# A pipelined attention kernel: where the probabilities are normalised, the row shape of two groups of matmuls, another order and prologue

## The chip, the core and the metric

One core of a Trainium2 chip. The number is the device time of one execution in microseconds; for the kernel before it is the median of three runs.

## The reference, cut to what matters

Two layers on 128 sequences of 64 rows and 256 features, all in float32. What the change touches:

```
x_mod = rms(x) * (1 + scale_a) + shift_a ;  q, k, v = split(x_mod @ qkv_w)
q, k  = rope(rms(q)), rope(rms(k))
attn  = softmax(q k^T / 4)                      # 16 heads of 16 features, 64 x 64
x    += gate_a * ((attn @ v) @ proj_w + proj_b)
x    += gate_m * ((silu(h @ w1) * (h @ w3)) @ w2)        # 704 hidden features
self  = [x, cond] @ W_self + b_self             # cond left out for rows whose sum is 0
out   = self + two graph attentions (20 keys, masked, with an edge bias)
y     = x + relu(out)
```

## The kernel before

A block is four sequences (256 rows, two tiles of 128); there are 32. Each engine runs its own list of steps (ORDER, line 83 on) once an iteration; an entry `(a, step, n)` works on block m + a, so three blocks ahead are under way at once. The lists are unrolled for the first iterations (-3 to 0) and the last three, and looped by `Fori` for 28 in between (`run_steps`). Engines meet by semaphores alone: `wait` for data, `wait_free` for a PSUM bank whose last reader must have gone. BANK says which of the eight PSUM banks each step writes.

Products with weights take three float32r terms for float32's precision: high part by low weight, high by high, low by high. ACT makes the high part (`nh`, `gh`, `aoh`), POOL or DVE the low one (`nl`, `gl`, `aol`); all these matmuls are issued at L486.

First attention, per tile: `score` (L587) into four banks, DVE takes the row maximum (L1151) and subtracts it (L1156), ACT makes the exponential (L897), PE transposes the unnormalised probabilities eight times (`probs_t`, L607), ACT copies them (L904, L906), and `mix` (L622) multiplies by v. v has two columns of ones per pair of heads, so the sums come out beside the result; DVE inverts them (L1162) and scales (L1165) into `aon`, PE transposes that back to features by rows (`mix_t`, L631), and ACT and DVE split it for `proj`. The second attention sums and inverts ahead of its transposes (L1267, L1271, POOL's multiply L1379), and its mix (L806) gives features by rows directly.

The MLP's hidden features are five whole chunks of 128 and a half one. `mlp_down` takes four chunks first and then chunk five and the half one, whose three terms are matmuls on partitions 64 to 127 (L696). Then DVE multiplies by the gate (L1206), POOL adds the residual (L1360), ACT and POOL split it, and `self` follows; it ends in `self_cond`, two matmuls of `cond_rows` (8 partitions) with `gate` (8 partitions, L1212).

POOL also does the first norm's root and power (L1303, L1305), the scaling by the modulation, the block-diagonal keys (L1327) and the residual of the first layer (L1356).

The prologue (line 1004 on) makes the modulation and the condition's product on PE into banks 0 to 3, splits the latter on DVE (L1065, L1067), and makes the rope tables; PE and POOL start their lists only after `mods_set` has reached 6, which is that split.

## Time and profile before

| | |
|---|---|
| median of 3 runs | 1424.35 us (1419.06 to 1425.61) |
| profiled execution | 1418.18 us, span 1416.1 us |
| PE busy | 1342.2 us, 95% |
| DVE busy | 1135.2 us, 80% |
| ACT busy | 878.6 us, 62% |
| POOL busy | 712.1 us, 50% |
| TensorE clock granted | 0.977 of full speed on average |

The span runs from the first to the last instruction. Busy is the union of the instructions' times of one engine; a matmul's time includes its way through the array, so neighbouring matmuls overlap, and what one costs is seen from start to start.

### The profile page before, as it was taken

How to read it: one execution, taken by the hardware profiler on the slowest of the kernel's cores; microseconds unless marked ns; L12 is line 12 of the kernel's file. 1: busy time of each engine (PE TensorE's matmuls, PEld its weight loads, DVE VectorE, ACT ScalarE, POOL GpSimd, SP SyncE). 2: the span in 40 equal slices, each digit the busy share in tenths (PEclk: the TensorE clock that was granted, in tenths of full speed). 3: DMA queues.
4: the chain of work that ended last, by engine and by line, in shares of the span. 5: the costliest groups of instructions: out<-in, count | busy, mean ns of one | idle time of the engine just before them, and what ended most of it. 6: DMA issues, size and time to landing. Idle time of an engine off the chain costs nothing.

```text
span 1416.1 us, 51305 instructions
## 1 busy us (share of the span) xinstructions
PE 1342.2 (95%) x20276; PEld 1229.1 (87%) x20276; DVE 1135.2 (80%) x2033; ACT 878.6 (62%) x1752; POOL 712.1 (50%) x612
## 2 busy tenths in 40 slices
PE   4679999999999999999999999999999999999985
PEld 3578899999998999999898999999999999999974
DVE  5667888888888888888888888888888888888753
ACT  4556666666666666666666666666666666656542
POOL 0235555455655544555555455555545555554541
PEclk8589999999999999999999999999999999999998
DMA  7001111010111101111110111111011111100100
GB/s 240 29 23 30 45 43 43 18 38 30 43 43 43 43 15 36 34 43 43 43 43 15 35 35 43 43 43 43 15 33 37 43 43 43 43 15 28 30 22 16
DMA packets 49827, 56.19 MB, mean 40 GB/s; under 512 B 4352, under 2 KB 47744, under 8 KB 49792
## 3 DMA queue, kind: packets, MB, share of 16 engines
q1 hardware_dynamic: 48944, 53.86, 12.1%
q10 hardware_dynamic: 848, 1.84, 0.4%
q8 instruction: 25, 0.41, 0.1%
q14 instruction: 10, 0.08, 0.0%
...
## 4 chain that ended last, share of the span: by engine, by line
PE 73%; issue 9%; POOL 7%; ACT 3%; DVE 1%; ACTq 0%; POOLq 0%; DVEq 0%
PE psum L486 39%; PE psum L607 5%; PE psum L622 5%; PE psum L728 4%; PE psum L792 4%; PE psum L758 4%; PE psum L775 3%; POOL nl L1315 3%; PE psum L587 3%; PE psum L806 2%; POOL gl L1315 2%; POOL kbd L1327 2%; ACT gh L926 1%; PE psum L534 1%; ACT qkT L892 1%
## 5 line engine op out<-in xcount | busy, mean ns | idle before, releaser
L1315 POOL TENSOR_TENSOR gl<-gf,gh 128x512 fp32r<-128x512 f32 x96 | 124.3, 1295 | 260.4 <-ACT gh L926 260.4
L486 PE MATMUL psum<-nh,w_lo 128*128 128x256 f32 x704 | 182.2, 289 | 0.0
L486 PE MATMUL psum<-nh,w_hi 128*128 128x256 f32 x704 | 176.8, 282 | 0.0
L1315 POOL TENSOR_TENSOR nl<-xn,nh 128x512 fp32r<-128x512 f32 x64 | 99.2, 1551 | 127.3 <-ACT nh L864 127.3
L486 PEld LDWEIGHTS psum<-nh,w_lo 128*128 128x128 f32 x704 | 132.8, 189 | 1.0 <-issue 1.0
L486 PEld LDWEIGHTS psum<-nh,w_hi 128*128 128x128 f32 x704 | 133.0, 189 | 0.0
L1379 POOL TENSOR_TENSOR e<-e,inv 128x640 f32<-128x640 f32 x64 | 82.0, 1282 | 87.6 <-DVE inv L1271 87.6
L486 PE MATMUL psum<-nl,w_hi 128*128 128x256 f32 x704 | 115.4, 282 | 0.0
L926 ACT ACTIVATE gh<-gf 128x512 fp32r<-128x512 f32 x96 | 60.3, 628 | 61.6 <-DVE gf L1201 60.8
L486 PEld LDWEIGHTS psum<-nl,w_hi 128*128 128x128 f32 x704 | 97.5, 188 | 0.0
L486 PE MATMUL psum<-qkv_lo,nh 128*128 128x512 f32 (+1 forms) x256 | 88.5, 356 | 2.8 <-ACT nh L864 2.8
L946 ACT ACTIVATE sf<-psum,colb 128x256 f32<-128x256 f32 x64 | 26.8, 470 | 103.3 <-PE psum L486 103.3
L1151 DVE TENSOR_REDUCE mx<-psum 128x16 f32<-128x1024 f32 x64 | 78.1, 1221 | 14.4 <-PE psum L587 14.1
L911 ACT ACTIVATE aoh<-psum 128x512 fp32r<-128x512 f32 x32 | 19.1, 598 | 109.2 <-PE psum L631 109.2
L486 PE MATMUL psum<-gh,w_lo 128*128 128x256 f32 x320 | 83.0, 290 | 1.3 <-ACT gh L926 1.3
L486 PE MATMUL psum<-qkv_hi,nh 128*128 128x512 f32 (+1 forms) x256 | 82.4, 343 | 0.0
L607 PE MATMUL psum<-ident,e 128*128 128x128 f32 x512 | 77.9, 289 | 4.3 <-ACT e L897 4.2
L1360 POOL TENSOR_TENSOR x<-x 128x512 f32<-128x512 f32 x32 | 41.5, 1296 | 78.2 <-DVE x L1206 78.2
L1327 POOL TENSOR_TENSOR kbd<-qkT,hmask 128x512 f32<-128x512 f32 x64 | 66.5, 1041 | 28.0 <-ACT qkT L892 28.0
L486 PE MATMUL psum<-gh,w_hi 128*128 128x256 f32 x320 | 79.6, 279 | 0.0
L1156 DVE TENSOR_TENSOR e<-psum,mx 128x1024 f32<-128x1024 f32 x64 | 78.0, 1218 | 1.3
L622 PEld LDWEIGHTS psum<-vb,pT 128*64 128x64 f32 x2048 | 66.6, 140 | 12.8 <-issue 12.5
...
## 6 DMA issues: line engine op xcount, KB each, us to landing
...
```

The lines of the kernel that those rows point to most:

```text
L486: last = nc.tensor.matmul(out, lhsT, rhs, start=start and i == 0, stop=stop and i == len(terms) - 1)
L607: last = nc.tensor.transpose(pT_out[t][j // 4][:, j % 4, :], e0[t][:, 2 * pair(j):2 * pair(j) + 2, :].rearrange("p h s -> p (h s)"), ident ...
L622: last = nc.tensor.matmul(mix_ps[t][s * S:(s + 1) * S, j, :], pT0[:, j, s * S:(s + 1) * S], vb[:, t, s, j, :], start=True, stop=True, tile ...
L728: last = nc.tensor.matmul(k1_out[:, k, :].rearrange("p (b k) -> p b k", b=MB), wk1[:, c, k * P:(k + 1) * P], sf[:, c, :].rearrange("p (b s ...
L758: last = nc.tensor.matmul(v1_out[r * NKP:(r + 1) * NKP, b, :], kv[:, c, b, :], wo1[:, c, r * P:(r + 1) * P], start=c == 0, stop=c == DC - ...
L792: last = nc.tensor.transpose(pT1_out[t][j // 4][:, j % 4, :], e1[t][:, 2 * pair(j):2 * pair(j) + 2, :, :].rearrange("p h a k -> p (h a k)" ...
L926: nc.scalar.activation(gh[:, 2 * n:2 * n + 2, :], gf[:, :, :], ACT.Copy).then_inc(g_hi.sem, 1)
L1151: nc.vector.tensor_reduce(mx0_v, s_v[t], AX.X, ALU.max).then_inc(maxima.sem, 1)
L1156: nc.vector.tensor_tensor(e0_v[t], s_v[t], mx0_v.unsqueeze(3).to_broadcast([P, NG, 4, S]), ALU.subtract).then_inc(shifted_s.sem, 1)
L1315: return nc.gpsimd.tensor_tensor(out, full, hi.bitcast(F32), ALU.subtract)
L1327: nc.gpsimd.tensor_tensor(kbd[:, t, :, :, :, :].rearrange("p c s h k -> p (c s) h k"), qkT[t][:, 1, :, :].rearrange("p c (s k) -> p (c s) ...
L1379: nc.gpsimd.tensor_tensor(e_v, e_v, inv1[t][:, :].unsqueeze(2).to_broadcast([P, ND * H, NKV]), ALU.mult)\
```

## The change

The first attention's exponentials are summed on DVE and inverted (`soft0`, `soft0_inverse`), POOL multiplies them in place, and PE transposes the finished probabilities; ACT copies the transposes over `e0`, so each tile has its own buffer, and waits for all eight transposes first. `mix` has the second attention's form: output by features, the transposes of `mix_t` and the two columns of ones are gone. The MLP's half chunk holds the low part of g in its first 64 partitions (POOL writes it there) and w2's last 64 rows twice, so its terms are ordinary matmuls on 128 partitions. `gate` and `cond_rows` have 128 partitions, the rest of them zero. The second attention's score bias is one instruction a tile. Banks and the orders of all engines are different. In the prologue PE and POOL no longer wait for the condition's split ahead of the lists, and DVE makes it and the tables behind the first block's shift. The diff, cut (of the old orders, PE's and POOL's stand):

```diff
-    "xT": 6, "qk": (2, 3), "v": (7, 1), "heads": (7, 5), "probsT": (5, 4, 4, 0), "probsT1": (0, 5, 4, 7),
-    "mix": (5, 6), "q1": (4, 6), "score": 0, "score1": 0, "mixT": 6, "proj": 2, "norm1": 7, "up": (6, 4, 6),
-    "gate": (3, 1, 0), "down": 1, "rowsum": 3, "self": 4, "k1": 5, "v1": 7, "mix1": 5,
+    "xT": 2, "qk": (6, 3), "v": (4, 1), "heads": (0, 2), "probsT": (3, 4, 0, 5), "probsT1": (7, 1, 3, 4),
+    "q1": (0, 4), "score": 3, "score1": 1, "proj": 1, "norm1": 7, "up": (5, 7, 4), "gate": (6, 3, 0), "down": 5,
+    "rowsum": 7, "self": 0, "k1": 1, "v1": 0, "mix1": 6, "mix": 2,
...
     "PE": [
-        (2, "heads", 1), (1, "proj", 0), (0, "self", 0), (0, "self_cond", 0), (2, "score", 0), (0, "k1", 0),
-        (0, "q1", 0), (1, "norm1_mean", 0), (0, "q1", 1), (1, "norm1_apply", 0), (2, "probsT", 0),
-        (3, "norm0_apply", 0), (0, "score1", 0), (0, "v1", 0), (2, "mix", 0), (2, "probsT", 1), (1, "mlp_up", 0),
-        (1, "mlp_up", 1), (3, "qkv", 0), (0, "probsT1", 0), (2, "mix", 1), (3, "qkv", 1), (0, "mix1", 0),
-        (0, "probsT1", 1), (1, "mlp_up", 2), (0, "mix1", 1), (1, "mlp_down", 0), (1, "mlp_down", 1), (2, "mixT", 0),
-        (3, "heads", 0),
+        (2, "heads", 1), (0, "mlp_down", 1), (1, "proj", 0), (2, "score", 0), (0, "self", 0), (0, "self_cond", 0),
+        (3, "norm0_apply", 0), (1, "norm1_mean", 0), (0, "k1", 0), (0, "q1", 0), (1, "norm1_apply", 0), (0, "q1", 1),
+        (0, "v1", 0), (0, "score1", 0), (1, "mlp_up", 0), (2, "probsT", 0), (1, "mlp_up", 1), (2, "probsT", 1),
+        (3, "qkv", 0), (2, "mix", 0), (2, "mix", 1), (3, "qkv", 1), (1, "mlp_up", 2), (0, "probsT1", 0),
+        (1, "mlp_down", 0), (0, "probsT1", 1), (3, "heads", 0), (0, "mix1", 0), (0, "mix1", 1),
     ],
     "DVE": [
...
+        (1, "norm1_mean", 0), (3, "norm0_apply", 0), (2, "score", 1), (0, "k1", 0), (2, "soft0", 0),
+        (1, "norm1_apply", 0), (2, "soft0_inverse", 0), (1, "norm1_shift", 0), (3, "norm0_shift", 0), (2, "soft0", 1),
+        (1, "edges", 0), (2, "soft0_inverse", 1), (0, "score1_bias", 0), (0, "score1_bias", 1), (0, "score1_max", 0),
+        (1, "mlp_up", 0), (0, "score1", 0), (0, "score1_max", 1), (0, "score1", 1), (0, "soft1", 0),
+        (0, "soft1_inverse", 0), (1, "mlp_up", 1), (3, "qkv", 0), (0, "soft1", 1), (0, "soft1_inverse", 1),
+        (3, "qkv", 1), (1, "mlp_up", 2), (3, "rope_scale", 0), (3, "rope", 0), (3, "rope", 1), (2, "mixT", 0),
+        (0, "mix1", 0), (0, "out", 0), (1, "mlp_down", 0), (1, "edge_masks", 0), (2, "proj", 0), (3, "score_max", 0),
+        (1, "row_mask", 0), (3, "score", 0), (2, "norm1_squares", 0), (3, "score_max", 1),
     ],
     "Activation": [
...
+        (0, "x2_split", 0), (3, "norm0_mean", 0), (1, "norm1_mean", 0), (0, "self", 0), (0, "self_split", 0),
+        (0, "keys", 0), (2, "score", 0), (0, "q1", 0), (2, "score", 1), (0, "q1", 1), (1, "norm1_apply", 0),
+        (3, "norm0_apply", 0), (1, "mlp_up", 0), (0, "v1", 0), (2, "probsT", 0), (1, "mlp_split", 0),
+        (0, "score1", 0), (1, "mlp_up", 1), (1, "edges", 0), (2, "probsT", 1), (0, "score1", 1), (3, "qkv", 0),
+        (1, "mlp_split", 1), (3, "qkv", 1), (2, "mixT", 0), (1, "mlp_up", 2), (3, "rope_scale", 0), (0, "probsT1", 0),
+        (1, "mlp_split", 2), (0, "probsT1", 1), (3, "heads", 0), (3, "heads", 1),
     ],
     "Pool": [
-        (1, "proj", 0), (0, "self_split", 0), (3, "norm0_mean", 0), (1, "norm1_mean", 0), (1, "norm1_scale", 0),
-        (3, "norm0_scale", 0), (1, "norm1_apply", 0), (3, "norm0_apply", 0), (0, "soft1", 0), (1, "mlp_up", 0),
-        (0, "soft1", 1), (1, "edges", 0), (1, "mlp_up", 1), (1, "mlp_up", 2), (1, "mlp_down", 0), (3, "heads", 0),
-        (1, "x2_split", 0), (3, "heads", 1),
+        (0, "mlp_up", 2), (2, "heads", 0), (2, "heads", 1), (0, "mlp_down", 0), (0, "x2_split", 0), (1, "proj", 0),
+        (3, "norm0_mean", 0), (3, "norm0_scale", 0), (0, "self_split", 0), (1, "norm1_mean", 0),
+        (1, "norm1_scale", 0), (1, "norm1_apply", 0), (2, "soft0", 0), (2, "soft0", 1), (3, "norm0_apply", 0),
+        (1, "mlp_up", 0), (1, "edges", 0), (0, "soft1", 0), (1, "mlp_up", 1), (0, "soft1", 1),
     ],
     "SP": [
-        (0, "self", 0), (3, "norm0_mean", 0), (1, "mlp_up", 0), (3, "norm0_scale", 0), (2, "norm0_apply", 0),
+        (1, "norm0_apply", 0), (3, "norm0_mean", 0), (1, "mlp_up", 0), (0, "self", 0), (3, "norm0_scale", 0),
         (0, "out", 0),
...
-        inv0 = [sb(f"inv0_{i}", [P, NJ, 2]) for i in range(TILES)]
-        aon = [sb(f"aon{i}", [P, NJ, 2, DH]) for i in range(TILES)]
+        sum0 = sb("sum0", [P, H])
+        inv0 = [sb(f"inv0_{i}", [P, H]) for i in range(TILES)]
         pT = sb("pT", [P, 2, NJ, P])
-        pT0, pT1 = pT[:, 0, :, :], pT[:, 1, :, :]
+
+        pT0 = [v[:, :, :].rearrange("p h s -> p (h s)").rearrange("p (j t) -> p j t", t=P) for v in e0]
+        pT1 = [pT[:, t, :, :] for t in range(TILES)]
...
+        mods_banks = [bank for i, bank in enumerate(banks) if i != BANK["xT"]][:4]
...
-        mix_ps = [banks[b][:, 0:NJ * (2 * DH + 2)].rearrange("p (j f) -> p j f", j=NJ) for b in BANK["mix"]]
-        aoT_ps = banks[BANK["mixT"]]
+        mix_ps = halves(BANK["mix"])
+        aoT_ps = banks[BANK["mix"]]
...
-            pe.wait_ge(mods_set.sem, 6)
-            pe.wait_ge(mods_set_a.sem, NMOD - 4)
...
+                if isinstance(m, int) and m == 0:
+                    pe.wait_ge(mods_set.sem, 6)
+                    pe.wait_ge(mods_set_a.sem, NMOD - 4)
...
-                wait(pe, exps, m, t + 1)
+                wait(pe, probs0, m, t + 1)
...
-                        last = nc.tensor.matmul(mix_ps[t][s * S:(s + 1) * S, j, :], pT0[:, j, s * S:(s + 1) * S],
-                                                vb[:, t, s, j, :], start=True, stop=True, tile_position=(0, s * S))
+                        f = 32 * (j % 4)
+                        last = nc.tensor.matmul(mix_ps[f:f + 32, j // 4, t * P + s * S:t * P + (s + 1) * S],
+                                                vb[:, t, s, j, :], pT0[t][:, j, s * S:(s + 1) * S],
+                                                start=True, stop=True, tile_position=(0, f))
                 last.then_inc(mixed.sem, 1)
-
...
-            def mix_t(m, n):
-                wait(pe, mix_normed, m, TILES)
-                wait_free(pe, m, (z_silu, -1, 3), (mix_normed, 0, 2))
-                for c in range(DC):
-                    for t in range(TILES):
-                        last = nc.tensor.transpose(aoT_ps[:, c * MT + t * P:c * MT + (t + 1) * P],
-                                                   aon[t][:, c * 4:(c + 1) * 4, :, :].rearrange("p j h f -> p (j h f)"),
-                                                   ident[:, :])
-                last.then_inc(aoT_done.sem, 1)
...
                     linear(down_ps[:, o, :], low_terms("w2", out_chunks[o], gl, [MC - 2]), False, False)
+
                 for o in both:
-                    for i, (w, a) in enumerate(((wl["w2"], gh), (wh["w2"], gh), (wh["w2"], gl))):
-                        last = nc.tensor.matmul(down_ps[:, o, :], w[half, MC - 1, out_chunks[o]], a[half, MC - 1, :],
-                                                start=False, stop=o == DC - 1 and i == 2, tile_position=(HALF, 0))
+                    last = linear(down_ps[:, o, :], high_terms("w2", out_chunks[o], gh, [MC - 1]), False, o == DC - 1)
                 last.then_inc(down_done.sem, 1)
 
...
-                wait(act, pT_ps, m, 2 * t + 1)
-                wait(act, mixed, m, t)
-                nc.scalar.activation(pT0[:, 0:4, :], pT_out[t][0], ACT.Copy).then_inc(pT_a.sem, 1)
                 wait(act, pT_ps, m, 2 * t + 2)
-                nc.scalar.activation(pT0[:, 4:8, :], pT_out[t][1], ACT.Copy).then_inc(pT_b.sem, 1)
+                nc.scalar.activation(pT0[t][:, 0:4, :], pT_out[t][0], ACT.Copy).then_inc(pT_a.sem, 1)
+                nc.scalar.activation(pT0[t][:, 4:8, :], pT_out[t][1], ACT.Copy).then_inc(pT_b.sem, 1)
 
             def mix_t(m, n):
...
+            def cond_and_tables():
+                dve.wait_ge(mods_ps.sem, NMOD + 1)
+                nc.vector.tensor_copy(cond_hi[:, :], mods_banks[3][:, 0:D]).then_inc(mods_set.sem, 1)
+                dve.wait_ge(mods_set.sem, 5)
+                nc.vector.tensor_tensor(cond_lo[:, :], mods_banks[3][:, 0:D], cond_hi[:, :].bitcast(F32), ALU.subtract).then_inc(mods_set.sem, 1)
+                dve.wait_ge(mods_set.sem, 6)
+                dve.wait_ge(sines.sem, 1)
...
+                low_parts(*LOW_PARTS["norm0_shift", 0])
...
-            def mix(m, t):
-                wait(dve, mixed, m, t + 1)
-                nc.vector.reciprocal(inv0[t][:, :, :], mix_ps[t][:, :, 2 * DH:2 * DH + 2]).then_inc(inv_sums.sem, 1)
-                wait(dve, inv_sums, m, t + 1)
-                wait_last(dve, aoT_done, m)
-                nc.vector.tensor_tensor(aon[t][:, :, :, :], mix_ps[t][:, :, 0:2 * DH].rearrange("p j (h f) -> p j h f", h=2),
-                                        inv0[t][:, :, :].unsqueeze(3).to_broadcast([P, NJ, 2, DH]), ALU.mult)\
-                    .then_inc(mix_normed.sem, 1)
+            def soft0(m, t):
+                wait(dve, exps, m, t + 1)
+                wait(dve, inv_sums, m, t)
+                nc.vector.tensor_reduce(sum0[:, :], e0[t][:, :, :], AX.X, ALU.add).then_inc(sums0.sem, 1)
+
+            def soft0_inverse(m, t):
+                wait(dve, sums0, m, t + 1)
+                nc.vector.reciprocal(inv0[t][:, :], sum0[:, :]).then_inc(inv_sums.sem, 1)
 
             def mix_t(m, n):
...
-                for a in range(ND):
-                    nc.vector.tensor_tensor(
-                        e1[t][:, :, a, 0:NKV].rearrange("p (r h) k -> p r h k", r=NG),
-                        s1_ps[t].rearrange("p r (a h k) -> p r a h k", a=ND, k=NKV)[:, :, a, :, :],
-                        edge_bias[:, t, a * NKV:(a + 1) * NKV].unsqueeze(1).unsqueeze(1).to_broadcast([P, NG, 4, NKV]), ALU.add)\
-                        .then_inc(biased1.sem, 1)
+                nc.vector.tensor_tensor(
+                    e1[t][:, :, :, 0:NKV].rearrange("p (r h) a k -> p r h a k", r=NG), s1_v[t],
+                    edge_bias[:, t, :].rearrange("p (a k) -> p a k", a=ND).unsqueeze(1).unsqueeze(1).to_broadcast([P, NG, 4, ND, NKV]),
+                    ALU.add).then_inc(biased1.sem, 1)
...
-            pool.wait_ge(mods_set.sem, 6)
...
-                low_part(gl[:, 2 * n:2 * n + 2, :], gf[:, :, :], gh[:, 2 * n:2 * n + 2, :]).then_inc(g_lo.sem, 1)
+                if n < MC // 2 - 1:
+                    low_part(gl[:, 2 * n:2 * n + 2, :], gf[:, :, :], gh[:, 2 * n:2 * n + 2, :]).then_inc(g_lo.sem, 1)
+                else:
+
+                    low_part(gl[:, 2 * n, :], gf[:, 0, :], gh[:, 2 * n, :]).then_inc(g_lo_whole.sem, 1)
+                    wait(pool, g_lo_whole, m, 1)
+                    low_part(gh[0:HALF, 2 * n + 1, :], gf[HALF:, 1, :], gh[HALF:, 2 * n + 1, :]).then_inc(g_lo.sem, 1)
+                    wait(pool, g_lo, m, n + 1)
...
+            def soft0(m, t):
+                wait(pool, inv_sums, m, t + 1)
+                nc.gpsimd.tensor_tensor(e0[t][:, :, :], e0[t][:, :, :], inv0[t][:, :].unsqueeze(2).to_broadcast([P, H, S]), ALU.mult)\
+                    .then_inc(probs0.sem, 1)
...
-        "w2": np.insert(a["L0_cond_w2_w"], [HM - HALF] * HALF, 0, 0),
+        "w2": np.concatenate([a["L0_cond_w2_w"], a["L0_cond_w2_w"][HM - HALF:]], 0),
```

## Rows read from the trace of the kernel before

**Rows 1.** The page: busy us, share of the span, instructions.

```profile
PE 1342.2 (95%) x20276; PEld 1229.1 (87%) x20276; DVE 1135.2 (80%) x2033; ACT 878.6 (62%) x1752; POOL 712.1 (50%) x612
```

**Rows 2.** Windows: busy us (instructions) of each engine, clock, DMA share, GB/s.

```profile
701.20:742.60 41.40, 41.13 (x635) 37.68 (x633) 34.78 (x63) 26.96 (x54) 22.34 (x20) 1.00 0.12 36
```

**Rows 3.** PE's time line over one block: start us, us, line, instruction.

```profile
701.17 0.38 PE L541 MATMUL psum<-ident,rms_inv 128*128 128x128 f32 x2
...
706.22 1.13 PE L622 MATMUL psum<-vb,pT 128*64 128x34 f32 x32
707.28 1.32 PE L607 MATMUL psum<-ident,e 128*128 128x128 f32 x8
...
720.60 0.81 PE L806 MATMUL psum<-pT,vb 128*32 128x64 f32 x32
721.33 1.09 PE L792 MATMUL psum<-ident,e 128*128 128x128 f32 x8
...
742.55 0.38 PE L541 MATMUL psum<-ident,rms_inv 128*128 128x128 f32 x2
```

**Rows 4.** The same time line, from the MLP's tail to k1.

```profile
729.05 0.38 PE L696 MATMUL psum<-gh,w_lo 64*128 64x256 f32 x1
...
729.92 0.66 PE L631 MATMUL psum<-ident,aon 128*128 128x128 f32 x4
730.42 1.04 PE L570 MATMUL psum<-ident,qr 128*128 128x128 f32 x8
731.43 0.38 PE L486 MATMUL psum<-aoh,proj_lo 128*128 128x256 f32 x1
...
733.02 0.50 PE L486 MATMUL psum<-nh,ones_r 128*128 128x256 f32 x2
...
734.20 0.28 PE L486 MATMUL psum<-nh,self_hi 128*128 128x256 f32 x1
734.59 0.50 PE L486 MATMUL psum<-nl,ones_r 128*128 128x256 f32 x2
734.93 0.64 PE L486 MATMUL psum<-nl,self_hi 128*128 128x256 f32 x4
735.68 0.49 PE L486 MATMUL psum<-gate,cond_rows 8*128 8x256 f32 x2
736.22 1.20 PE L587 MATMUL psum<-kbd,qkT 32*64 32x128 f32 x64
737.34 2.01 PE L728 MATMUL psum<-sf,wk 128*128 128x80 f32 x16
```

**Rows 5.** DVE's groups: busy us, mean ns of one, idle before and releaser.

```profile
L1151 DVE TENSOR_REDUCE mx<-psum 128x16 f32<-128x1024 f32 x64 | 78.1, 1221 | 14.4 <-PE psum L587 14.1
...
L1248 DVE TENSOR_TENSOR e<-psum,edge_bias 128x320 f32<-128x320 f32 x128 | 56.3, 482 | 8.3 <-PE psum L775 8.3
...
L1165 DVE TENSOR_TENSOR aon<-psum,inv 128x256 f32<-128x256 f32 x64 | 27.2, 424 | 2.4 <-DVE inv L1162 0.2
...
L1162 DVE RECIPROCAL inv<-psum 128x16 f32<-128x16 f32 x64 | 16.3, 254 | 49.0 <-PE psum L622 48.8
```

**Rows 6.** Time line of DVE and POOL behind the MLP's end, same block.

```profile
730.24 0.68 DVE L1206 TENSOR_TENSOR x<-psum,mods 128x512 f32<-128x512 f32 x1
...
731.00 1.29 POOL L1360 TENSOR_TENSOR x<-x 128x512 f32<-128x512 f32 x1 [2.45 <-DVE x L1206]
...
739.97 0.95 POOL L1305 TENSOR_TENSOR rms_inv<-rms_root,minus_half 128x2 f32<-128x2 f32 x1
```

**Rows 7.** POOL's groups: its multiply of the second attention.

```profile
L1379 POOL TENSOR_TENSOR e<-e,inv 128x640 f32<-128x640 f32 x64 | 82.0, 1282 | 87.6 <-DVE inv L1271 87.6
```

**Rows 8.** L1130 alone over one block: ns min/median/max, first and last start.

```profile
L1130 DVE TENSOR_TENSOR qr<-qc,qs x4: 410/416/1024, 720.9 to 724.4; 128x256 f32<-128x256 f32 x4
```

**Rows 9.** Time line of POOL and DVE at its first two.

```profile
720.30 1.29 POOL L1315 TENSOR_TENSOR gl<-gf,gh 128x512 fp32r<-128x512 f32 x1 [1.36 <-ACT gh L926]
720.85 1.36 DVE L1130 TENSOR_TENSOR qr<-qc,qs 128x256 f32<-128x256 f32 x2
```

**Rows 10.** Time line: POOL's first instruction of its list.

```profile
19.67 0.20 POOL L1303 TENSOR_TENSOR rms_root<-x_ms,eps 128x2 f32<-128x2 f32 x1 [19.22 <-DVE cond_lo L1067]
```

More of the change, by code:

```diff
@@ L88 @@
     ],
     "DVE": [
-        (2, "rope", 0), (2, "rope", 1), (0, "mlp_down", 0), (1, "mixT", 0), (1, "proj", 0), (0, "row_mask", 0),
-        (0, "edge_masks", 0), (2, "score_max", 0), (2, "score", 0), (1, "norm1_squares", 0), (2, "score_max", 1),
[4 rows of a table removed]
-        (1, "mlp_up", 1), (2, "mix", 1), (3, "qkv", 0), (3, "qkv", 1), (1, "mlp_up", 2), (0, "mix1", 0),
-        (1, "edges", 0), (3, "rope_scale", 0), (0, "out", 0),
[5 rows of a table added]
+        (3, "qkv", 1), (1, "mlp_up", 2), (3, "rope_scale", 0), (3, "rope", 0), (3, "rope", 1), (2, "mixT", 0),
@@ L98 @@
+        (0, "mix1", 0), (0, "out", 0), (1, "mlp_down", 0), (1, "edge_masks", 0), (2, "proj", 0), (3, "score_max", 0),
+        (1, "row_mask", 0), (3, "score", 0), (2, "norm1_squares", 0), (3, "score_max", 1),
     ],
     "Activation": [
-        (2, "rope_scale", 0), (0, "mlp_split", 2), (1, "mixT", 0), (2, "heads", 0), (2, "heads", 1),
-        (0, "x2_split", 0), (0, "self", 0), (1, "norm1_mean", 0), (0, "keys", 0), (0, "self_split", 0),
-        (3, "norm0_mean", 0), (2, "score", 0), (0, "q1", 0), (0, "q1", 1), (2, "probsT", 0), (2, "score", 1),
@@ L509, in _ @@
             for c in range(DC):
-                last = nc.tensor.matmul(banks[3][:, 0:D], cond[:, c, :], w_cond[:, c, :], start=c == 0, stop=c == DC - 1)
+                last = nc.tensor.matmul(mods_banks[3][:, 0:D], cond[:, c, :], w_cond[:, c, :], start=c == 0, stop=c == DC - 1)
             last.then_inc(mods_ps.sem, 1)
@@ L811, in _ @@
             run_steps(pe, "PE", {
-                "norm1_mean": norm1_mean, "norm0_apply": norm0_apply, "norm1_apply": norm1_apply, "qkv": qkv, "heads": heads, "score": score, "probsT": probs_t, "mix": mix, "mixT": mix_t, "proj": proj,
+                "norm1_mean": norm1_mean, "norm0_apply": norm0_apply, "norm1_apply": norm1_apply, "qkv": qkv, "heads": heads, "score": score, "probsT": probs_t, "mix": mix, "proj": proj,
                 "mlp_up": mlp_up, "mlp_down": mlp_down, "self": self_feat, "self_cond": self_cond, "k1": k1,
@@ L1011, in _ @@
             nc.vector.memset(vb1[:, :, :, :].rearrange("p b f j -> p (b f j)"), 0.0).then_inc(zeros_set.sem, 1)
+            for v in (gate, cond_rows):
+                last = nc.vector.memset(v[:, :].bitcast(F32), 0.0)
+            last.then_inc(zeros_set.sem, 1)
             for v in e1:
                 last = nc.vector.memset(v[:, :, :, :].rearrange("p h a k -> p (h a k)"), 0.0)
-            last.then_inc(zeros_set.sem, 1)
-            dve.wait_ge(zeros_set.sem, 5)
-            for h in range(2):
-                last = nc.vector.memset(vb[h * S:(h + 1) * S, :, :, :, 2 * DH + h:2 * DH + h + 1], 1.0)
             last.then_inc(zeros_set.sem, 1)
@@ L1112, in _ @@
             half = DH // 2
+            def cond_and_tables():
[5 more added lines that the diff above has]
+                dve.wait_ge(sines.sem, 1)
+                for i in range(2):
+                    for a in range(2):
+                        nc.vector.tensor_tensor(cosw[:, i, a * half:(a + 1) * half], lnw[:, i, a * half:(a + 1) * half],
+                                                ang[:, 1, :], ALU.mult)
+                        last = nc.vector.scalar_tensor_tensor(sinw[:, i, a * half:(a + 1) * half], ang[:, 0, :],
+                                                              (1.0, -1.0)[a], lnw[:, i, a * half:(a + 1) * half],
+                                                              ALU.mult, ALU.mult)
+                last.then_inc(table_step.sem, 1)
+                dve.wait_ge(table_step.sem, 9)
+                low_parts(*LOW_PARTS["norm0_shift", 0])
             def qkv(m, t):
@@ L1153, in score @@
             def score(m, t):
-                wait(dve, pT_ps, m, 2 * (t + 1 - TILES))
+                wait(dve, mixed, m, t + 1 - TILES)
                 wait(dve, maxima, m, t + 1)
@@ L1333, in norm0_scale @@
             def norm0_scale(m, n):
+                if isinstance(m, int) and m == 0:
+                    pool.wait_ge(mods_set.sem, 4)
                 wait(pool, xT_in_s, m, 16)
```

152 lines of the change are left out of this document (66 added, 86 removed), and 4 rows, old and new, of the table ORDER.

## The prediction, made before the changed kernel ran

> **What bounds the kernel now.** I read the page's busy line first: PE is busy 95% of the span, DVE 80%, POOL 50% [rows 1]. That alone doesn't say that PE is the limit, because ends of matmuls are modelled. So I read the table by windows in the middle: in 41.40 us PE is busy 41.13, DVE 34.78, ACT 26.96, POOL 22.34 at full granted clock [rows 2]. Then the time line of PE: the same instruction of two successive blocks (L541) starts at 701.17 and at 742.55, so one block of four sequences takes 41.38 us [rows 3], and between those two marks PE issues almost without a hole. The other engines have about 6.6 us (DVE) or more to spare in every block. The kernel is thus 32 times 41.4 us of PE's instruction stream plus about 92 us of filling and draining the pipeline. What takes PE instructions away pays one for one, as long as nothing that PE waits for comes later than its turn.
>
> PE's pace is read from a group in the time line: four matmuls of 256 columns in 0.64 us, one alone 0.28, so (0.64 - 0.28) / 3 = 0.12 us from start to start [rows 4].
>
> **What the change takes off PE, per block.**
> (a) The transposes of the mixed output (mixT) go: L631 starts at 729.92 and what follows it at 730.42 [rows 4]: 0.50 us.
> (b) The mix keeps its 16 matmuls a tile but takes the form that the second attention's mix has already (32-column weights, 64 moving columns). The old form runs from 706.22 to 707.28 = 1.06 us, the form taken over from 720.60 to 721.33 = 0.73 us [rows 3]. Twice 0.33 = 0.66 us.
> (c) The tail of the MLP's second product: six matmuls on 64 rows run from 729.05 to 729.92 = 0.87 us [rows 4]; four on whole rows at PE's pace are 0.48: 0.39 us. Entering and leaving the 64-row form costs something on top, see below; I take 0.47.
> (d) The condition's matmuls on 8 rows: 735.68 to 736.22 = 0.54 us for two instructions whose pace gives 0.24 [rows 4]. Whatever follows has an entry too, so I take 0.20 of the 0.30 (bounds 0 and 0.30).
> Sum 1.83 us. In (c) and (d) the time line shows that a group with another number of rows starts and ends some 0.1 us late. The Trainium skill says why (TensorEngine Tiling (Array Packing), Key Properties): a change of the tiling mode drains the engine. By that rule the new order should give a little more, since it also puts the two mixes of each attention side by side (two pairs of switches fewer); I leave that out of the sum.
> Before, PE also stood still twice in this stretch: the pace puts the low ones_r matmuls at 734.32 and they start at 734.59; four matmuls from 734.93 should end at 735.41 and the gated ones start at 735.68 [rows 4]. That is 0.54 us. PE without any wait would then take 41.38 - 0.54 - 1.83 = 39.0 us a block.
>
> **What it puts on the other engines, per block.**
> DVE: two reciprocals and two multiplies of the old normalisation go, 2 x (0.254 + 0.424) = 1.36 us. Two sums of 128x1024 come; the nearest row is the maximum over the same shape, 1.221 us, and the two reciprocals are 0.254 again: 2.95 us [rows 5]. The sum reads SBUF and not PSUM; bounds 1.1 and 1.3 each. The bias of the second attention becomes one instruction of 640 elements instead of two of 320 at 0.482; in between the rows of 256 and 1024 elements (0.424 and, for 1024, 1.221) it is about 0.82: -0.3 us for both tiles (bounds -0.5 and +0.3, as its reading of PSUM has more dimensions). DVE goes from 34.8 to 36.1 us.
> POOL: two multiplies of 128x1024 by a broadcast column. The same operation at 640 elements takes 1.282 us [rows 7], so 2.05 by its rate (bounds 1.3 and 2.6). With the split of one low part in two, about +4.2 us: 22.3 becomes 26.5.
> ACT: its copies of the transposed probabilities are the same in number and size: nothing. SP: the order of five loads changes, all small beside the block; no cost.
> Both rises are hidden as long as DVE (36.1) and POOL (26.5) stay under PE, with 3 to 4 us to spare on DVE where there were 6.6.
>
> The cover is not free of traps, because POOL and DVE disturb each other. L1130, two halves of the rotation, takes 0.410 us at best and 1.024 at worst in the same block; the long one starts at 720.85, inside a POOL subtraction that runs from 720.30 to 721.59 [rows 8, 9]. The Trainium skill's SBUF page (SBUF — State Buffer, Who interferes with whom) has the rule: a DVE instruction with two SBUF inputs and a GpSimd instruction that reads SBUF exclude each other for the whole instruction. Here the trace agrees. By it the two new POOL multiplies of 2.05 us each can hold up such a DVE instruction for up to 2.05 us. By the same rule the new sums (one input) are never held up. In the new order POOL runs them after the first part of norm1's low parts, while DVE has mostly sums, maxima and PSUM readers; the first DVE operation with two SBUF inputs behind them is the subtraction in score1, which I expect to be held up by under 1 us. That eats DVE's reserve and not PE's time.
>
> **Where PE will wait.** I followed the new orders from one mlp_down to the next. In most places what PE needs is 0.4 to 3 us early (probabilities of tile 0: about 1.2 us early; rope before heads: little, but early). One stretch is not covered. Old order between the last product of the MLP and k1: mixT, heads, proj, self, self_cond, score. New order: proj, score, self, self_cond, norm0_apply (block 3 ahead), norm1_mean, k1. Count from the start s of the last tail matmul.
> The chain to self: PE's end and hand-over 0.33, DVE 0.68, POOL's addition 1.29, ACT's split; POOL starts at 731.00, its end is 732.29, and PE's self starts at 733.02 [rows 4, 6], so ACT and the hand-overs are 0.73. With 0.08 between DVE and POOL self can start at s + 3.11. PE has only proj (731.43 to 733.02, 1.59) and score (736.22 to 737.34, 1.12) [rows 4] and the tail matmul's 0.12 to do: s + 2.83. Wait 0.28, as heads no longer stand there.
> The chain to self_cond: rowsum's low matmuls end, DVE compares, PE gets the gate: 734.59 to 735.68 before, 1.09; PE has the 0.34 + 0.48 of its own [rows 4]: wait 0.27, as before.
> The chain to norm0_apply: on POOL, behind x2's low part (1.24), come the residual's addition (as the 1.29 of rows 6, 1.24 from start to start) and the root and power of norm0, about 0.3 and 0.95 [rows 6]; the power is less where DVE leaves the port free. From s + 3.1: 3.1 + 1.24 + 1.24 + 0.3 + (0.7 to 0.95) = s + 6.6 to 6.8. PE has finished self_cond at s + 5.75 (3.11, high parts 1.30, low parts and gate 1.09, two matmuls 0.24). Wait 0.85 to 1.1. k1 is just ready after it.
> Sum of waits 1.4 to 1.65; block 39.0 + 1.5 = 40.5, and 40.3 if the spared switches count. I take 40.4: 1.0 us less than now.
>
> **Filling and draining.** POOL's first instruction waits until 19.67 us for the condition's low part [rows 10]; afterwards it waits only for what it reads, and PE can spread at once behind its first matmuls (about 18.7). So the first normalised block is some 2 us earlier. Against that, in the filling blocks the sum, the reciprocal and POOL's multiply (1.2 + 0.25 + 2.05) stand on the open chain where before 0.25 + 0.42 and the transposes did. I take -2 for the filling (bounds -5 and +4) and -1 for the draining.
>
> **Sum.** The loop's 28 blocks and the one ahead of it: 29 x 1.0 = 29 us, and 3 more: 32 off. The profiled execution took 1418.18 us (span 1416.1): 1386 for its like. It lies 6.2 under the median of the runs, 1424.35, so the median should be about 1392.
>
> **Rivals.**
> Dense: the waits don't come (POOL reaches norm0's root earlier, or x2's chain is faster than I have it). Then a block takes 39.0 and 29 x 2.4 + 3 = 72 us go: 1352. For it: rows 3 and 4 show how little PE waits today although the same engines feed it. Against: the chain to norm0_apply is made of durations that are all in the trace. Chance 0.18.
> Nothing: a second unforeseen wait of about 1 us a block stands beside the three (the likeliest is probabilities of the first tile: POOL's 2.05 at its upper bound, held up by DVE's shifts): 40.4 + 1.0, so 1420 to 1424. Chance 0.08.
> Slower: DVE becomes the bound. Its 6.6 us without work may be waits that stay, and not a reserve, and work of 1.3 us plus up to 2.05 us of being shut out by POOL's two multiplies, once a block, come on top: 34.8 + 6.6 + 1.3 + 0.9 to 2.05 = 43.6 to 44.8, at least 2 us a block over now, 29 x 2.2 = 64: 1488. In a mild form, where half of the idle time is used, 1440. The point from which it decides is DVE over 41.4 us a block. For it: L1130 [rows 8]. Against: DVE's idle pieces are many and most of its new work stands in front of them. Chance 0.10.
> My own case has 0.64.
>
> **The numbers.** The range from 1352 to 1418 leaves out about 1 in 10 on each side. This kernel's measurement can tell about 0.5% (7 us) from no change: faster 0.82, same 0.08, slower 0.10.
>
> **What would show it.** In the changed profile L541's like repeats every 40.4 us; the mix takes 0.73, the tail 0.5; no L631; PE waits once for the power of norm0 (0.85 to 1.1) and once for x2's split (0.3); DVE 36.1 of 40.4 and POOL 26.5. Wrong: a repeat under 39.5 (my chain is too long), over 41 (a wait that I don't see), or DVE without any idle time.

## Result: slower, 1457.8 us against a forecast of 1392

The changed kernel takes 1457.78 us (median of 4 runs, 1448.58 to 1460.17) where the kernel before takes 1423.18: a ratio of 1.0235 (95% interval 1.0191 to 1.0279). The forecast was 1392 us, its range ended at 1418. The change makes the kernel slower, clear of no change. The profiled execution has a span of 1446.5 us instead of 1416.1; it is the fastest of the changed kernel's, so the loss read from it below is rather too small.

The page of the changed kernel, busy line (compare [rows 1]):

```profile
PE 1313.8 (91%) x20084; PEld 1236.7 (85%) x20084; DVE 1210.0 (84%) x1969; ACT 884.6 (61%) x1752; POOL 836.3 (58%) x708
```

PE has less to do, as forecast, and is a smaller share of a longer span. The chain of work that ended last, with its shares of the span, names on its page what wasn't there before:

```profile
PE 74%; DMA 7%; DVE 4%; issue 3%; ACT 1%; POOL 1%; SPq 1%; DVEq 0%; ACTq 0%; POOLq 0%
PE psum L492 44%; PE psum L723 7%; DMA cond_rows<-cond_parts 6%; PE psum L753 4%; PE psum L787 4%; PE psum L614 4%; PE psum L770 3%; PE psum L801 3%; PE psum L628 2%; PE psum L577 2%; DVE edge_v L1222 2%; ACT sf L937 1%; DVE edge_n L1223 1%; SPq L464 1%; PE psum L545 1%
```

A DMA of 8 KB, the condition's rows, stands on the chain. Of PE's waits between 300 and 1100 us (who waited for whom: us in total, times, longest) it is the largest:

```profile
PE psum L492 <- DMA cond_rows<-cond_parts: 26.5, 19, 1.7
```

That is 1.4 us a block. The time line of PE around it (start, duration, instruction, idle time before and releaser; compare [rows 4]):

```profile
788.62 0.63 PE L492 MATMUL psum<-aol,proj_hi 128*128 128x256 f32 x4
789.18 1.21 PE L594 MATMUL psum<-kbd,qkT 32*64 32x128 f32 x64
790.75 0.50 PE L492 MATMUL psum<-nh,ones_r 128*128 128x256 f32 x2 [0.36 <-ACT nh L929]
...
792.12 0.50 PE L492 MATMUL psum<-nl,ones_r 128*128 128x256 f32 x2
792.46 0.64 PE L492 MATMUL psum<-nl,self_hi 128*128 128x256 f32 x4
794.65 0.50 PE L492 MATMUL psum<-gate,cond_rows 128*128 128x256 f32 x2 [1.55 <-DMA cond_rows<-cond_parts]
794.99 0.38 PE L530 MATMUL psum<-ident,rms_inv 128*128 128x128 f32 x2
795.21 0.50 PE L538 MATMUL psum<-mean_col,x_sq 128*128 128x1 f32 x4
796.16 3.52 PE L723 MATMUL psum<-sf,wk 128*128 128x80 f32 x16 [0.45 <-ACT sf L937]
```

The gated matmuls (`self_cond`, operands `gate` and `cond_rows`) wait for their rows until 794.65, though the gate itself is ready at about 793.1 (DVE's instruction runs from 792.66 for 0.41). And k1, the last line, takes 3.52 us where it took 2.01: PE's clock has gone down. The windows of the same stretch show it (columns as in [rows 2]; the number before the DMA share is the granted clock, 0.50 is 1.2 GHz):

```profile
785.00:792.00 7.00, 6.54 (x152) 6.06 (x144) 5.87 (x11) 1.59 (x3) 5.08 (x5) 1.00 0.40 118
792.00:795.00 3.00, 1.45 (x11) 1.12 (x10) 2.69 (x5) 1.54 (x5) 2.21 (x4) 1.00 0.70 227
795.00:799.40 4.40, 3.95 (x24) 3.87 (x23) 2.65 (x4) 4.11 (x6) 3.67 (x4) 0.66 0.00 0
799.40:803.00 3.60, 3.60 (x19) 3.60 (x19) 2.60 (x6) 0.64 (x2) 0.29 (x1) 0.50 0.00 0
```

PE is busy for less than half of the 3 us in which it waits, then the clock falls to its lower level. This happens in nearly every block: 22 times between 160 and 1250 us, 123 us in all (counted from the granted clock in the packed trace); before, never in that stretch. The same view of 800 us, the kernel before and the changed one:

```profile
300.00:1100.00 800.00, 794.18 (x12182) 727.93 (x12181) 671.81 (x1200) 521.64 (x1048) 429.75 (x366) 1.00 0.12 36
300.00:1100.00 800.00, 758.20 (x11657) 715.62 (x11657) 700.37 (x1129) 509.96 (x1017) 489.84 (x414) 0.94 0.12 36
```

Why the load is late is in SP's time line:

```profile
787.84 0.40 SPq L480 DMA_DIRECT2D out_T<-y  x1
788.76 0.37 SPq L460 DMA_DIRECT2D x_res<-in_xT  x1
789.39 0.37 SPq L452 DMA_DIRECT2D x_in<-in_x  x1
790.27 0.37 SPq L464 DMA_DIRECT2D adj<-in_adj  x1
790.84 0.30 SPq L475 DMA_DIRECT2D cond_rows<-cond_parts  x1
```

SP takes its steps in order. The store of y waits for DVE, then the residual, x and the edges go out, and only then the condition's rows, 3.0 us behind the store, 2.3 us ahead of the moment at which PE could use them, and behind 950 KB of other loads. Most of the 3.0 us is the issuing itself, 0.6 to 0.9 us from one to the next; the edges also wait for the edge masks on DVE, which is 0.3 us a block:

```profile
SPq L464 <- DVE edge_n L1223: 2.7, 9, 0.3
```

In the kernel before the rows were issued first behind the store, 0.9 us behind it and 5.5 us ahead of their use:

```profile
729.28 0.40 SPq L474 DMA_DIRECT2D out_T<-y  x1
730.19 0.30 SPq L469 DMA_DIRECT2D cond_rows<-cond_parts  x1
730.75 0.37 SPq L446 DMA_DIRECT2D x_in<-in_x  x1
737.00 0.37 SPq L458 DMA_DIRECT2D adj<-in_adj  x1
```

The edges wait for the masks there for 5.6 us a block, but the rows stood ahead of that wait.

A block's length is read below from the first and the last gated matmul of a stretch (two a block, so 38 of them span 18 blocks). Before: x38 from 321.6 to 1067.2, so 745.6 / 18 = 41.4 us. After:

```profile
L492 PE MATMUL psum<-gate,cond_rows x38: 276/332/387, 324.4 to 1093.7; 128*128 128x256 f32 x38
```

769.3 / 18 = 42.74 us; the forecast was 40.4. These lengths come from one profiled execution each, and the runs of a kernel differ by 0.2% to 1.3%, so a few tenths of a us a block between two kernels are not safe by themselves.

### The profile page after: what moved, and what is told of

It is laid out like the page before. It is cut to its first block, busy times and chain, and to the rows that moved or that the text cites. A ratio compares the mean times of both kernels' runs of the same rounds, so it can differ in the third digit from the quotient of the medians.

```text
span 1446.5 us, 50657 instructions
## 1 busy us (share of the span) xinstructions
PE 1313.8 (91%) x20084; PEld 1236.7 (85%) x20084; DVE 1210.0 (84%) x1969; ACT 884.6 (61%) x1752; POOL 836.3 (58%) x708
## 4 chain that ended last, share of the span: by engine, by line
PE 74%; DMA 7%; DVE 4%; issue 3%; ACT 1%; POOL 1%; SPq 1%; DVEq 0%; ACTq 0%; POOLq 0%
PE psum L492 44%; PE psum L723 7%; DMA cond_rows<-cond_parts 6%; PE psum L753 4%; PE psum L787 4%; PE psum L614 4%; PE psum L770 3%; PE psum L801 3%; PE psum L628 2%; PE psum L577 2%; DVE edge_v L1222 2%; ACT sf L937 1%; DVE edge_n L1223 1%; SPq L464 1%; PE psum L545 1%
## 5 line engine op out<-in xcount | busy, mean ns | idle before, releaser
L1307 POOL TENSOR_TENSOR gl<-gf,gh 128x512 fp32r<-128x512 f32 (+1 forms) x96 | 109.8, 1144 | 221.4 <-ACT gh L917 221.4
L1379 POOL TENSOR_TENSOR e<-e,inv 128x1024 f32<-128x1024 f32 x64 | 121.0, 1912 | 6.7 <-DVE inv L1162 6.7
L723 PE MATMUL psum<-sf,wk 128*128 128x80 f32 x512 | 94.8, 362 | 11.2 <-ACT sf L937 11.1
L957 ACT ACTIVATE q1T<-psum,bq 128x256 f32<-128x256 f32 x128 | 53.7, 470 | 80.8 <-PE psum L492 80.8
L492 PE MATMUL psum<-gh,w_lo 128*128 128x256 f32 x384 | 102.7, 296 | 0.0
L723 PEld LDWEIGHTS psum<-sf,wk 128*128 128x128 f32 x512 | 88.7, 269 | 13.7 <-issue 11.3
L908 ACT ACTIVATE th<-psum 128x512 f32<-128x512 f32 x64 | 38.2, 598 | 97.9 <-PE psum L492 97.9
L492 PE MATMUL psum<-nh,q_lo 128*128 128x256 f32 x256 | 93.6, 381 | 0.0
L492 PE MATMUL psum<-nh,q_hi 128*128 128x256 f32 x256 | 84.5, 346 | 0.0
L1254 DVE TENSOR_TENSOR e<-e,mx 128x640 f32<-128x640 f32 x64 | 79.9, 1248 | 1.1
```

The costliest lines, as they stand in the source:

```text
L492: last = nc.tensor.matmul(out, lhsT, rhs, start=start and i == 0, stop=stop and i == len(terms) - 1)
L723: last = nc.tensor.matmul(k1_out[:, k, :].rearrange("p (b k) -> p b k", b=MB), wk1[:, c, k * P:(k + 1) * P], sf[:, c, :].rearrange("p (b s ...
L957: last = nc.scalar.activation(q1T[:, direction, o, :], q1_out[direction][:, o, :], ACT.Identity, bias=bq4[:, k:k + 1], scale=DH ** -0.5)
L1254: nc.vector.tensor_tensor(e1_v[t], e1_v[t], mx1[:, :].unsqueeze(2).to_broadcast([P, ND * H, NKV]), ALU.subtract)\
L1307: return nc.gpsimd.tensor_tensor(out, full, hi.bitcast(F32), ALU.subtract)
L1379: nc.gpsimd.tensor_tensor(e0[t][:, :, :], e0[t][:, :, :], inv0[t][:, :].unsqueeze(2).to_broadcast([P, H, S]), ALU.mult)\
```

## Experiments

Theory A: the late load makes PE wait, and the wait takes the clock down, so that both go with the load in time. Rival R1: the other waits take the clock down anyway. Rival R2: DVE and POOL with the new work bound the block. Every run is compared with runs of the kernel before on the same chip (1421.5 to 1423.1 us).

**cond_ahead**

```diff
-        (1, "norm0_apply", 0), (3, "norm0_mean", 0), (1, "mlp_up", 0), (0, "self", 0), (3, "norm0_scale", 0),
+        (1, "norm0_apply", 0), (3, "norm0_mean", 0), (1, "mlp_up", 0), (3, "norm0_scale", 0), (1, "self", 0),
```

> The changed kernel with SP's order alone altered: the load of the condition's rows for the next block is issued behind the loads of this one (it waits only for the last reader), a whole block ahead of its use. Theory A (PE waits for this late load, and the idle time takes the clock down): the wait of 1.6 us and the half-clock stretch go, PE's wait ahead of norm0_apply of about 0.9 us appears instead; a block takes 40.1 us, the kernel 1375 to 1400 us. Rival R1 (the clock falls for the other waits anyway): the block loses 1.0 us only, 1425 to 1432 us, granted clock stays near 0.93. Rival R2 (DVE and POOL, with the new multiply, are the bound): 1450 to 1460 us.

Measured: 1408.99 us, ratio 0.9917 (0.9889 to 0.9944); a block 773.9 / 19 = 40.73 us. One entry moved in SP's list takes 49 us off and turns the change into a gain. It is 9 us above what A gave; the clock still fell in about half of the blocks (12 times, 57 us at the lower level between 160 and 1250 us). PE's waits in 300 to 1100 us (in total, times, longest):

```profile
PE psum L530 <- POOL rms_inv L1297: 18.4, 20, 1.3
PE psum L492 <- ACT nh L929: 7.1, 20, 0.4
PE psum L492 <- POOL nl L1307: 0.8, 3, 0.3
```

The wait for norm0's power that was forecast at 0.85 to 1.1 us a block is there, 18.4 / 20 = 0.92.

**cond_first**: `(0, "self", 0)` put first in SP's list, so that the rows go out right behind the store of y.

> The changed kernel with the load of the condition's rows put first in SP's list, ahead of the three other loads, so that it is issued right behind the store of y, some 5 us ahead of its use. Theory A: as good as a whole block ahead, within 5 us of that run. If it is the DMA queue's backlog and not the place in SP's order that makes it late, it stays over 1440 us. R2: 1450 to 1460 us.

Measured: 1426.02 us, ratio 1.0035 (1.0010 to 1.0061): A's expectation failed. The rows come in time here too, no wait names them; but the issue of one more load stands ahead of x's for the first norm, about 0.6 us, and the wait for norm0's power is longer (1.24 us a block) and three blocks in four lose clock (20 falls, 98 us at the lower level, a block 41.57 us):

```profile
PE psum L530 <- POOL rms_inv L1297: 23.6, 19, 1.4
```

SP's order decides over two chains, the rows and x. That the 0.6 us alone makes it is not separated from the clock. The second reading that was on record here, that the other transfers make the load late, isn't fully ruled out either: from issue to use the rows took 3.8 us in the changed kernel (790.84 to 794.65) and 2.8 in before_late below, where one load stands just ahead. But in cond_first the rows go out 0.9 us behind the store (734.55 and 733.64) instead of 3.0, and the 2.1 us between are more than the wait was, so the place in the list is enough to explain it.

**fill_wait**

```diff
+                for _ in range(14):
+                    nc.tensor.matmul(banks[BANK["mix"]][:, 0:MT], ones_r[:, 0:P], nl[1][:, 0, :], start=True, stop=True)
                 wait(pe, row_gate, m, 1)
                 wait(pe, cond_rows_s, m, 16)
```

> The changed kernel with 14 more matmuls of 256 columns ahead of the wait for the condition's rows, into a PSUM bank that nobody reads: PE waits as long as before for the load, but busy. If the clock's fall costs about 2 us a block on top of the wait, it goes to 1390 to 1410 us though work was added; if the clock costs nothing, 1455 to 1475 us.

Measured: 1395.80 us, ratio 0.9817 (0.9790 to 0.9845). The load is as late as in the changed kernel, PE has more to do, and the kernel is 62 us faster. A block takes 766.9 / 19 = 40.36 us, 2.4 less than 42.74, and the granted clock is 1.00:

```profile
300.00:1100.00 800.00, 782.97 (x12732) 742.06 (x12732) 733.54 (x1192) 541.65 (x1073) 516.88 (x437) 1.00 0.12 38
```

So the clock alone is more than the loss against the kernel before: with the late wait and a full clock the change is a gain. The Trainium skill (TensorE: Matmul & The Clock Gate, Terms) puts the penalty at about the time at the lower clock times one minus the granted share, here one half. As an estimate by that, the 123 us over 25.5 blocks are 4.8 us a block and cost 2.4, and the runs agree. Over the whole kernel, from the first gated matmul to the last, the two differ less, 42.0 against 40.4 us a block, as the changed kernel also has blocks in which the clock stays up.

**before_late**: in the kernel before, `(0, "self", 0)` moved behind `(1, "mlp_up", 0)` in SP's list; nothing else.

> The kernel before with the load of the condition's rows put behind the load of the edges in SP's list, as the change has it; nothing else. In the profile of before the edge load is issued at 737.0 of a block whose gated matmuls start at 735.7, so the rows would land about 741. Theory A: PE waits about 5 us a block and loses clock as well, 1424 + 32 x (5 to 8) = 1585 to 1680 us. R2 (the load's place costs nothing by itself): 1424 us.

Measured: 1660.54 us, ratio 1.1682 (1.1615 to 1.1750), a block 737.0 / 15 = 49.1 us, in the range that A gave. PE waits 5 us a block for the rows, and between 160 and 1250 us the clock is at its lower level for 219 us:

```profile
PE psum L486 <- DMA cond_rows<-cond_parts: 78.7, 16, 5.2
```

The mechanism needs no part of the change but SP's order. Here it is the wait for the edge masks, which holds SP for about 6 us a block, that makes the load late; in the changed kernel it is mostly the loads issued ahead.

**ahead_filled**: cond_ahead with idle matmuls, whose result nobody reads (`fill`, in the loop only), 3 ahead of self, 2 ahead of self_cond, 7 ahead of norm0_apply.

> The kernel of run cond_ahead with idle matmuls (256 columns, into a free PSUM bank) in the loop ahead of PE's three remaining waits: 3 ahead of self, 2 ahead of self_cond, 7 ahead of norm0_apply. They take about as long as the waits do. Theory A': what cond_ahead still lost was clock (2.3 us a block were at half clock there), not time in the waits themselves: the clock stays full, a block takes 39.6 us and the kernel 1370 to 1385 us. Rival: the clock's fall came elsewhere and costs nothing on the path: 1405 to 1412 us.

Measured: 1377.09 us, ratio 0.9666 (0.9608 to 0.9724), a block 757.5 / 19 = 39.87 us. As expected: filling the waits takes 0.9 us a block off, so cond_ahead still lost about that to the clock, and R1 is right in this weaker form, that the three small waits, 1.5 us together, suffice in half of the blocks.

**root_early**: cond_ahead with norm0's squares, root and power earlier (the edit, cut).

```diff
-    SP:   (3, "norm0_mean", 0), ... (1, "self", 0), (0, "out", 0)
+    SP:   ... (1, "self", 0), (4, "norm0_mean", 0), (0, "out", 0)
-    ACT:  (0, "x2_split", 0), (3, "norm0_mean", 0)
+    ACT:  (3, "norm0_mean", 0), (0, "x2_split", 0)
-    Pool: (0, "mlp_down", 0), (0, "x2_split", 0), (1, "proj", 0), (3, "norm0_mean", 0)
+    Pool: (3, "norm0_mean", 0), (0, "mlp_down", 0), (0, "x2_split", 0), (1, "proj", 0)
```

> The kernel of run cond_ahead with norm0's squares, root and power ahead of the MLP's end instead of behind it (ACT: norm0_mean ahead of x2_split; POOL: norm0_mean ahead of mlp_down; SP: the load of x one iteration earlier). The prediction's chain to norm0_apply is then gone: PE's wait for the power (0.92 us a block) goes, k1 then waits about 0.5 us for self, so 0.4 us a block are gained directly and up to 1.1 more if the clock stays up: 1365 to 1397 us. If the power was not on the path: 1405 to 1412 us.

Measured: 1393.96 us, ratio 0.9803 (0.9766 to 0.9840), 40.54 us a block. The wait for the power is gone, two others have grown:

```profile
PE psum L492 <- ACT nh L929: 21.5, 20, 1.1
PE psum L538 <- DVE x_sq L1062: 13.4, 20, 0.7
```

The time is at the slow end of what was expected; the clock is better (24 us at the lower level instead of 57), but PE waits more in sum, 34.9 us in this stretch where cond_ahead's rows add up to 26.3.

**root_early_filled**: 3 idle matmuls ahead of self and 2 ahead of self_cond.

> The kernel of run root_early with 3 idle matmuls ahead of self and 2 ahead of self_cond. If root_early's clock still falls, this shows by how much: 1360 to 1375 us, about 39.3 us a block. If its clock is full anyway, the same as root_early within 5 us.

Measured: 1381.24 us, ratio 0.9724 (0.9690 to 0.9759), 760.9 / 19 = 40.05 us a block, no fall of the clock at all in the stretch; 6 us above the expected range, as waits of 1.2 us a block remain.

**root_mid**: as root_early, POOL's norm0_mean behind its mlp_down.

> As run root_early (load of the condition's rows ahead; squares of norm0 early on ACT, its load early on SP), but POOL's root and power of norm0 stand behind its addition of x2, where POOL waits 0.7 us for ACT anyway. In root_early they stood ahead of it and PE's wait for x2's high part rose from 0.37 to 1.1 us. If that was the cause, the wait is back at 0.4 to 0.6 us and the kernel is 10 to 25 us under root_early's 1394: 1368 to 1384 us. Otherwise 1390 to 1396.

Measured: 1398.33 us, ratio 0.9844 (0.9803 to 0.9886): the expectation failed. The wait for x2 is back at 0.35 us as expected, so a block should be shorter, but the clock falls in more blocks than in root_early (61 us against 24) and it takes 773.9 / 19 = 40.73 us. Fewer us of waiting (20.4 instead of 34.9), more us at the lower clock: the sum of the waits doesn't decide it, and which of them triggers the fall in a block isn't settled.

**root_mid_filled**: root_mid with 3 idle matmuls ahead of self, 2 ahead of self_cond, 5 ahead of norm1_mean.

> root_mid with idle matmuls in the loop: 3 ahead of self, 2 ahead of self_cond, 5 ahead of norm1_mean. If the clock is full without them, the same as root_mid or up to 6 us slower; if root_mid still loses clock, faster by that. The best that the waits allow is 39.3 us a block: 1355 to 1372 us.

Measured: 1367.54 us, ratio 0.9622 (0.9583 to 0.9661), 750.7 / 19 = 39.51 us a block. The fastest version, 3.8% under the kernel before and 6% under the changed one; its additions to PE compute nothing that is used:

```profile
300.00:1100.00 800.00, 795.33 (x12908) 750.30 (x12908) 741.45 (x1214) 546.67 (x1090) 530.12 (x449) 1.00 0.13 39
```

**multiply_small**: ahead_filled with `e0[t][:, :, 0:2]` in POOL's new multiply; it leaves out the normalisation of the other 62 columns and serves for the time alone.

> The kernel of run ahead_filled (1377 us) with POOL's multiply of the probabilities cut to 2 of 64 columns (it leaves the normalisation out for the others): POOL has some 3.7 us less a block and holds up no DVE instruction. If the multiply is hidden, as the prediction had it: within 5 us of ahead_filled. If POOL and its port bound the block (R2): 1340 to 1360 us.

Measured: 1375.45 us, ratio 0.9674 (0.9637 to 0.9710), 1.6 us from ahead_filled. POOL's busy time in 300 to 1100 us falls from 531.54 to 456.91 us and nothing follows: the multiply is hidden. R2, which had 1340 to 1360 us, falls.

**condition_8_rows**: ahead_filled with `cond_rows[0:2 * MB, ...]` and `gate[0:2 * MB, :]` as operands.

> The kernel of run ahead_filled with the condition's two matmuls on 8 partitions again. The prediction's term (d) says 0.2 us a block, so 6 us slower. In run before_whole_rows they took the same 0.54 us on 128 rows as before on 8, which says no difference: within 3 us.

Measured: 1377.75 us, ratio 0.9695 (0.9655 to 0.9735), 0.7 us from ahead_filled. That is within the 3 us expected, but it doesn't price the row shape: ahead_filled's own runs lie between 1365.7 and 1383.2 us, and what stands right behind these matmuls is a wait that can take up the difference. From start to start they take 0.43 us on 8 rows (711.24 to 711.67) where they took 0.33 on 128 (717.79 to 718.12 in ahead_filled), and PE's wait for norm0's power falls from 4.1 to 0.9 us in 300 to 1100 us.

**before_whole_rows**: the kernel before with the two changes of row shape alone (POOL's split low part, w2's rows twice, 128 partitions for `gate` and `cond_rows`).

> The kernel before, with its own order, banks and prologue, and only the two changes of row shape: the MLP's half chunk as whole-row matmuls (with its low part in the free half) and the condition's matmuls on 128 partitions. The prediction's terms (c) and (d), 0.47 + 0.20 us a block on a PE without gaps: 1424 - 21 = about 1400 us (1393 to 1412). If the split low part on POOL or another wait eats it: 1418 to 1426 us.

Measured: 1429.44 us, ratio 1.0053 (1.0034 to 1.0071): it is outside both ranges expected (1393 to 1412, or 1418 to 1426), a block takes 751.1 / 18 = 41.73 us. Its time lines of PE, DVE and POOL where the tail is:

```profile
736.12 0.28 PE L487 MATMUL psum<-gh,w_hi 128*128 128x256 f32 x1
736.45 0.50 PE L487 MATMUL psum<-gl,w_hi 128*128 128x256 f32 x2
...
737.26 0.60 PE L632 MATMUL psum<-ident,aon 128*128 128x128 f32 x4
...
740.91 0.50 PE L487 MATMUL psum<-nh,ones_r 128*128 128x256 f32 x2 [0.53 <-ACT nh L937]
...
743.57 0.50 PE L487 MATMUL psum<-gate,cond_rows 128*128 128x256 f32 x2
744.11 0.65 PE L588 MATMUL psum<-kbd,qkT 32*64 32x128 f32 x26
```

```profile
736.08 0.87 DVE L1283 SCALAR_TENSOR_TENSOR y<-sf,x 128x512 f32<-128x512 f32 x1
736.87 1.28 DVE L1142 TENSOR_TENSOR qr<-qr,qk_inv 128x512 f32<-128x512 f32 x2
738.07 0.68 DVE L1207 TENSOR_TENSOR x<-psum,mods 128x512 f32<-128x512 f32 x1
```

```profile
734.84 0.74 POOL L1316 TENSOR_TENSOR gl<-gf,gh 128x256 fp32r<-128x256 f32 x1 [5.67 <-ACT gh L925]
735.66 0.73 POOL L1316 TENSOR_TENSOR gh<-gf,gh 64x256 fp32r<-64x256 f32 x1
```

PE's tail is shorter (736.45 to 737.26 = 0.81; before, from the low terms at 728.65, 1.27). But the low part in two instructions is ready at 736.39 and holds PE's low terms up by 0.2 us; DVE's y, two SBUF inputs, runs beside POOL's second half and takes 0.87 (0.89 on average) instead of 0.62 (0.65); DVE comes to its multiply by the gate (L1207) at 738.07, 0.65 us behind PE's end, and self waits 0.53 for x2. So in the old order, as this block reads, the chain of rope, that multiply and x2 on DVE, POOL and ACT sets the time at this place, and PE's saving doesn't reach it. No run takes one link of this chain away.

## Why the prediction was wrong

The step that failed is one sentence: "SP: the order of five loads changes, all small beside the block; no cost." I counted the transfers' sizes and not when SP comes to issue them. The walk along the orders covered PE, DVE, ACT and POOL and left out SP, whose list had the one move that mattered: the condition's rows behind the residual, x and the edges, and all of them behind the store of y, which waits for DVE. So they were issued 3.0 us behind that store instead of 0.9, and PE waited for them for 1.4 us a block (26.5 / 19). With the load a block ahead the kernel takes 1408.99 instead of 1457.78 us (cond_ahead). The second thing, which the sum puts at nothing without a word, is the clock: it cost 2.4 us a block more. With that alone prevented (fill_wait) the same kernel is at 1396, 4 us from the forecast. This is luck: the load still comes late there, and the wait that it fills stands in for the wait for norm0's power that I had forecast, while PE's work is shorter than I had it. From PE's 38.2 us without waits (below), 2.2 of waiting and 2.4 for the clock make 42.8, the measured 42.74; no other term of this size is missing.

**Off PE.** (a) The transposes, 0.50: gone. (b) The mix: forecast 0.73 a tile; both tiles together take 1.10 us in the changed kernel's time line (773.95 to 775.05), so 1.02 are saved a block and not 0.66. The trace agrees with the drain at mode switches that the Trainium skill states (TensorEngine Tiling (Array Packing), Key Properties): two mixes side by side need one entry.

```profile
773.95 1.17 PE L628 MATMUL psum<-e,vb 128*32 128x64 f32 x64
775.05 0.50 PE L492 MATMUL psum<-qkv_lo,nh 128*128 128x512 f32 x1
```

(c) The tail: the second part of mlp_down runs from 786.41 to 787.67 = 1.26 us, 1.73 before (728.19 to 729.92): 0.47, exactly as taken. (d) The condition: 0.2 forecast, and its two matmuls do take 0.34 instead of 0.54 us in the changed kernel (794.65 to 794.99), but only half of it for the reason given. In the old order they take 0.54 on 128 rows as well (before_whole_rows, 743.57 to 744.11), where `score` follows; in the new order, where whole-row matmuls follow, 8 rows take 0.43 and 128 rows 0.33. So half of the gain belongs to what follows and not to the 8 rows. One saving has no term in my sum: the 16 transposes of the first attention's probabilities, from their start to the next group's, took 1.03 + 1.07 = 2.10 us a block before (701.40 to 702.43, and 707.28 to 708.35 behind a mix) and take 0.79 each in the changed kernel, 0.5 us less:

```profile
770.87 1.04 PE L614 MATMUL psum<-ident,e 128*128 128x128 f32 x8
771.66 0.48 PE L492 MATMUL psum<-qkv_lo,nh 128*128 128x512 f32 x1
```

How much of it is the mode switch beside them isn't separated. PE without waits is 38.2 us a block and not 39.0, as an estimate: ahead_filled's 39.87 less its 12 idle matmuls of 0.12 and 0.25 us of waits. The 0.36 us more of (b) and these 0.5 account for the difference.

**On the others.** DVE's sum 1211 ns and reciprocal 244, the bias 814, POOL's multiply 1912 (forecast 1221, 254, 820, 2050):

```profile
L1158 DVE TENSOR_REDUCE sum<-e 128x16 f32<-128x1024 f32 x64 | 77.5, 1211 | 0.1
L1242 DVE TENSOR_TENSOR e<-psum,edge_bias 128x640 f32<-128x640 f32 x64 | 49.4, 814 | 28.3 <-PE psum L770 28.3
L1254 DVE TENSOR_TENSOR e<-e,mx 128x640 f32<-128x640 f32 x64 | 79.9, 1248 | 1.1
L1379 POOL TENSOR_TENSOR e<-e,inv 128x1024 f32<-128x1024 f32 x64 | 121.0, 1912 | 6.7 <-DVE inv L1162 6.7
```

The third row is the hold-up forecast for score1's subtraction: 0.82 before, 1.25 on average now. With POOL's multiply cut down it falls from 1.13 to 0.94 (ahead_filled, multiply_small), and the time of the kernel stays: the hold-up doesn't reach PE.

**Where PE waits.** x2's split 0.28, measured 0.36; norm0's power 0.85 to 1.1, measured 0.92 in cond_ahead. With the load in time and the clock full the waits, filled, and the work make 39.9 (ahead_filled), 0.5 under my 40.4.

**Filling and draining.** The first normalised block came earlier (DVE's multiply at 19.69 instead of 21.83), but the first gated matmuls came at 114.2 us instead of 110.3, 2.9 us of that block waiting for the same late load, and the drain behind the last ones is 31.0 us instead of 28.9. So 6 us were lost there where I had 3 gained.

**The rivals.** The slower case had the right sign and the wrong engine: DVE is busy 37.6 us in a block of 43.6 (760.75 to 804.36) and bounds nothing. No rival held a wait in SP's queue.
